# Row maxima of an attention kernel: a double-buffered tile, a later transposition, and a copy and a split on two other engines

## What is computed

```python
h = _layernorm(x, axis=-1) * (1 + ca) + sa
Q = _lora_linear(h, Wq, bq, Aq, Bq).reshape(N, S, HEADS, HEAD_DIM)      # K, V alike
energy = jnp.einsum('nqhd,nkhd->nhqk', Q, K) / jnp.sqrt(jnp.float32(HEAD_DIM))
attn = jax.nn.softmax(energy, axis=-1)
out = jnp.einsum('nhqk,nkhd->nqhd', attn, V).reshape(N, S, EMBED)
...
```

## Time and profile before

| | us |
|---|---|
| median of 3 runs (lowest, highest) | 1998.48 (1993.88, 2003.48) |
| the profiled execution: its own time | 2001.02 |
| the profiled execution: span of its instructions | 1999.3 |
| mean granted TensorE clock | 0.978 of full speed |
| busy PE, DVE, ACT, POOL | 94%, 79%, 59%, 16% |

### The profile page before, as it was taken

How to read it: one execution, slowest core, us unless ns; L and a number is a source line. 1 busy time by engine, 2 the same in 40 slices (tenths; PEclk the granted TensorE clock), 3 DMA queues, 4 the chain that set the end, 5 groups by cost and what they waited for, 6 DMA issues and landing times.

```text
span 1999.3 us, 33500 instructions
## 1 busy us (share of the span) xinstructions
PE 1883.2 (94%) x12334; PEld 705.1 (35%) x12335; DVE 1576.3 (79%) x2802; ACT 1179.2 (59%) x1354; POOL 322.2 (16%) x361
## 2 busy tenths in 40 slices
PE   7688999999999999999999999999975799999997
PEld 5332222222222222222222222222224555666664
DVE  4377999999999999999999999999816632254443
ACT  4534777777777777777777777777761221111111
POOL 5535000000000000000000000000016532323332
PEclk9898999999999999999999999999997799999999
DMA  4541111211111111111111111111056433222221
GB/s 152 169 148 37 41 41 50 64 44 41 41 60 57 39 41 55 58 46 38 42 60 56 42 38 53 56 43 38 11 171 214 139 106 116 95 78 71 68 66 47
DMA packets 89734, 141.48 MB, mean 71 GB/s; under 512 B 13104, under 2 KB 60208, under 8 KB 89472
## 3 DMA queue, kind: packets, MB, share of 16 engines
q1 hardware_dynamic: 74336, 102.01, 16.2%
q0 software_dynamic: 10240, 32.40, 4.9%
q10 hardware_dynamic: 5024, 5.24, 0.8%
HBM read 90.84 MB, written 48.51 MB: 70 GB/s over the span
## 4 chain that ended last, share of the span: by engine, by line
PE 83%; DVE 4%; issue 4%; POOL 3%; DMA 3%; ACT 1%; SPq 1%; POOLq 0%; DVEq 0%; ACTq 0%
PE ps L853 25%; PE ps L842 21%; PE ps L808 16%; PE ps L1514 7%; PE ps L1065 5%; PE ps L1532 3%; PE ps L1398 3%; DVE mx L909 2%; DMA l_in<-inverse_sums 2%; POOL parts L693 1%; ACT prob L947 1%; POOL rest L689 1%; PE ps L1523 1%; DMA qk_parts<-parts 1%; POOL k_low L681 1%
## 5 line engine op out<-in xcount | busy, mean ns | idle before, releaser
L909 DVE TENSOR_REDUCE mx<-ps 128x1 f32<-128x512 f32 x2048 | 1276.8, 682 | 47.4 <-PE ps L808 42.9
L947 ACT ACTIVATE prob<-ps 128x1024 f32<-128x1024 f32 x1024 | 992.3, 1021 | 294.6 <-PE ps L842 292.3
L853 PE MATMUL ps<-prob,vs 128*32 128x512 f32 x4096 | 546.4, 605 | 0.7 <-ACT prob L947 0.7
L808 PE MATMUL ps<-k_high,q_high 64*128 64x512 bf16 x2048 | 411.9, 388 | 32.4 <-DMA k_low<-qk_parts 17.5
L842 PE MATMUL ps<-q_high,k_high 64*128 64x512 bf16 x2048 | 389.6, 377 | 3.4 <-ACT prob L947 2.5
L842 PE MATMUL ps<-q_low,k_low 34*128 34x512 bf16 x2048 | 389.8, 377 | 0.0
L808 PEld LDWEIGHTS ps<-k_high,q_high 64*128 64x128 bf16 x2048 | 100.9, 92 | 670.6 <-DVE mx L909 603.7
L975 POOL COPY vs<-v_all 128x256 f32 (+1 forms) x32 | 12.7, 400 | 1138.3 <-PE ps L853 1138.2
L842 PEld LDWEIGHTS ps<-q_low,k_low 34*128 34x128 bf16 x2048 | 100.0, 94 | 117.5 <-issue 0.3
L1563 ACT ACTIVATE esig<-ps 128x512 f32<-128x512 f32 x39 | 23.3, 597 | 195.9 <-PE ps L1514 195.9
L842 PEld LDWEIGHTS ps<-q_high,k_high 64*128 64x128 bf16 x2048 | 101.4, 96 | 86.9 <-ACT prob L947 27.9
(11 more groups left out here) (145 smaller groups left out, 1312.4 us busy)
## 6 DMA issues: line engine op xcount, KB each, us to landing
k_high<-qk_parts SPq DMA_DIRECT2D x128, 128.0 KB
qk_parts<-parts SPq DMA_DIRECT2D x32, 384.0 KB, 3.6
q_high<-qk_parts SPq DMA_DIRECT2D x128, 64.0 KB
k_low<-qk_parts SPq DMA_DIRECT2D x128, 64.0 KB
head_out<-head_out_sb SPq DMA_DIRECT2D x32, 256.0 KB, 10.8
sorted_in<-zero_row POOLq DMA_DIRECT2D x13, 390.0 KB, 7.0
xs<-sorted_in SPq DMA_DIRECT2D x39, 130.0 KB
q_low<-qk_parts SPq DMA_DIRECT2D x128, 32.0 KB
```

The costliest lines, as they stand in the source:

```text
L808: pe.matmul(ps[:, ring_bank(2 * m + u), :], q_high[p][mine, t * P:(t + 1) * P], k_high[p][mine, c * CH:(c + 1) * CH], start=True, stop=Tru ...
L853: mm = pe.matmul(ps[32 * j:32 * j + 32, 7, :], vs[buf(h)][:, kt, :], prob[:, kt % 2, j * CH:(j + 1) * CH], start=(kt == 0), stop=(kt == KT ...
L909: dve.tensor_reduce(mx[:, at, c:c + 1], ps[:, ring_bank(k), :], AX.X, ALU.max).then_inc(s_ring, 1)
L947: act.activation(prob[:, kt % 2, :].rearrange("p (u c n) -> p u c n", u=2, c=2)[:, :, half, :], ps[:, 2 * half:2 * half + 2, :], ACT.Exp). ...
```

## The change

- `mx` becomes two tiles, used by heads in turn. DVE reduces unit 0 and unit 1 of the next head first and makes `mneg` of the finished head after them; it doesn't wait there for a write of its own.
- The transposition of the maxima moves from between units 0 and 1 of the next head to behind its third pair (`TURN_AT` = 2). Its place in the ring moves with it: after units 4 and 5.
- ACT copies the turned maxima out of PSUM into a new tile `turned_sb` (`take_turned`), behind the exponentials of step 12, and counts `s_turned`, which frees the place in the ring. GpSimd makes both rows of `mb` from that tile (`split_maxima`) and counts `s_mb`, for which SP waits.
- `LEAD` is 12. Two more pairs of head 1 stand beside the matmuls ahead of the first head, and pairs 0 and 1 of a head stand in step 11 instead of 12. The turn stays in step 12.
- The waits of the ring come from a table, the class `Ring`. `max_pair` calls `ring_place` once for each of its two units, and each call writes a wait of its own.
- The gates on GpSimd are written in parts, with the split of head 1 between them; the staging of the values, the weight loads and the zero fills are written out by head, each set ahead of a split.

```diff
-LEAD = 10
+LEAD = 12
...
 RING = 3
+TURN_AT = 2
...
+class Ring:
+
+
+    def __init__(self):
+        self.place, self.released = {}, []
+        count = {"dve": 0, "act": 0}
+        for n in range(NH + 1):
+            for m in range(PAIRS if n < NH else 0):
+                for u in range(2):
+                    self.add((n, m, u), "dve", count)
+                if n and m == TURN_AT:
+                    self.add((n - 1, "turned"), "act", count)
+        self.add((NH - 1, "turned"), "act", count)
+        self.total = count
+
+    def add(self, what, engine, count):
+        self.place[what] = len(self.released)
+        count[engine] += 1
+        self.released.append((engine, count[engine]))
+
+    def bank(self, what):
+        return 4 + self.place[what] % RING
+
+    def made(self, what):
+        return self.place[what] + 1
+
+    def taken(self, what):
+        return self.released[self.place[what]][1]
...
-        mx = r("mx", [P, KT, CPB])
+        mx = buffers("mx", [P, KT, CPB], F32, r)
...
                 p = buf(h)
-                sp.wait_ge(s_ring, MAXIMA * (num(h) + 1) + (1 if last else 2))
+                sp.wait_ge(s_mb, num(h) + 1)
...
+        ring = Ring()
+
+        def ring_place(pe, what):
+
+            at = ring.place[what]
+            if at >= RING:
+                engine, n = ring.released[at - RING]
+                pe.wait_ge(s_ring if engine == "dve" else s_turned, n)
+            return ps[:, ring.bank(what), :]
 
         def max_pair(pe, h, m):
 
-            p, t, c = buf(h), m // CPB, m % CPB
-
-            def unit(u):
+            p, n, t, c = buf(h), num(h), m // CPB, m % CPB
+            if m == 0:
+                pe.wait_ge(s_stack[p], STACK * (nth(h) + 1))
+            banks = [ring_place(pe, (n, m, u)) for u in range(2)]
+            for u in range(2):
                 mine = slice(u * HROWS, (u + 1) * HROWS)
-                pe.matmul(ps[:, ring_bank(2 * m + u), :], q_high[p][mine, t * P:(t + 1) * P],
+                pe.matmul(banks[u], q_high[p][mine, t * P:(t + 1) * P],
                           k_high[p][mine, c * CH:(c + 1) * CH], start=True, stop=True).then_inc(s_max, 1)
 
-            if m:
-                pe.wait_ge(s_ring, MAXIMA * num(h) + item(2 * m + 1) - RING + 1)
-                unit(0)
-                unit(1)
-                return
-            pe.wait_ge(s_stack[p], STACK * (nth(h) + 1))
-            if not first_head(h):
-                pe.wait_ge(s_ring, MAXIMA * num(h) - 1)
-            unit(0)
-            if not first_head(h):
-                turn_maxima(pe, plus(h, -1))
-            unit(1)
-
         def turn_maxima(pe, h):
+            bank = ring_place(pe, (num(h), "turned"))
             pe.wait_ge(s_neg, num(h) + 1)
-            pe.transpose(ps[0:KT, TURNED_BANK, 0:P], mneg[:, :], ident[:]).then_inc(s_max, 1)
+            pe.transpose(bank[0:KT, 0:P], mneg[:, :], ident[:]).then_inc(s_max, 1)
...
                     scores(*this, 1)
                     if beside:
                         max_pair(pe, who, first)
-                    elif first == 0 and after == 1:
-                        turn_maxima(pe, plus(h, 1))
+                    if first == TURN_AT and num(who) <= NH:
+                        turn_maxima(pe, plus(who, -1))
                     weigh(h, kt - 1)
                     if beside:
                         max_pair(pe, who, first + 1)
...
                 for m in range(n * LEAD // 4, (n + 1) * LEAD // 4):
                     if m:
                         max_pair(pe, (0, 1), m)
+                    if m == TURN_AT:
+                        turn_maxima(pe, (0, 0))
...
-        def reduce_pair(dve, step, h, m):
-
-            t, c = m // CPB, m % CPB
+        def reduce_pair(dve, h, m):
+
+            n, t, c = num(h), m // CPB, m % CPB
             for u in range(2):
-                k = 2 * m + u
-                if k == 1 and not first_head(h):
-                    turned_maxima(dve, step, plus(h, -1))
-                dve.wait_ge(s_max, 2 if first_head(h) and k == 0 else MAXIMA * num(h) + item(k) + 1)
+                what = (n, m, u)
                 at = u * HT + t
-                dve.tensor_reduce(mx[:, at, c:c + 1], ps[:, ring_bank(k), :], AX.X, ALU.max).then_inc(s_ring, 1)
-
-        def turned_maxima(dve, step, h, last=False):
-            dve.wait_ge(s_max, MAXIMA * (num(h) + 1) + (1 if last else 2))
-            dve.wait_ge(s_mrows[buf(h)], 64 * (nth(h) + 1))
-            turned = ps[0:KT, TURNED_BANK, 0:P]
-            step(dve.tensor_copy(mb[buf(h)][:, 0, :], turned))
-            dve.tensor_tensor(mb[buf(h)][:, 1, :], turned, mb[buf(h)][:, 0, :],
-                              ALU.subtract).then_inc(s_ring, 1)
+                dve.wait_ge(s_max, ring.made(what))
+                dve.tensor_reduce(mx[n % 2][:, at, c:c + 1], ps[:, ring.bank(what), :], AX.X,
+                                  ALU.max).then_inc(s_ring, 1)
 
         def attend_vector(dve, step):
-            def head(h, pairs=range(1, PAIRS), last=False):
-
-                for m in pairs:
-                    reduce_pair(dve, step, h, m)
-                dve.wait_ge(s_ring, MAXIMA * (num(h) + 1))
-                dve.tensor_reduce(mneg[:], mx[:], AX.X, ALU.max, negate=True).then_inc(s_neg, 1)
-                if last:
-                    turned_maxima(dve, step, h, last)
-                else:
-                    dve.wait_ge(s_neg, num(h) + 1)
-                    reduce_pair(dve, step, plus(h, 1), 0)
-
-            for p in range(NB):
-                dve.sem_inc(s_mrows[p], 64)
-            head((0, 0), pairs=())
+            def negate(n):
+
+                dve.wait_ge(s_ring, ring.taken((n, PAIRS - 1, 1)))
+                dve.tensor_reduce(mneg[:], mx[n % 2][:], AX.X, ALU.max, negate=True).then_inc(s_neg, 1)
+
             for n in range(1, NH):
-                head((0, n), last=n == NH - 1)
+                for m in range(PAIRS):
+                    reduce_pair(dve, (0, n), m)
+                    if m == 0:
+                        negate(n - 1)
+            negate(NH - 1)
             invert(dve, 0)
...
+            def take_turned(n):
+
+                what = (n, "turned")
+                act.wait_ge(s_max, ring.made(what))
+                wait(act, s_mb, n)
+                act.copy(turned_sb[:], ps[0:KT, ring.bank(what), 0:P]).then_inc(s_turned, 1)
...
+                if c * LEAD // 4 <= TURN_AT < (c + 1) * LEAD // 4:
+                    take_turned(0)
...
                     exps(n, kt)
                     if n and kt == 0:
                         head_copy(n - 1)
+                    if n + 1 < NH and LEAD + 2 * (kt - 1) == PAIRS + TURN_AT:
+                        take_turned(n + 1)
...
+            def split_maxima(n):
+
+                p = n % NB
+                pool.wait_ge(s_turned, n + 1)
+                pool.wait_ge(s_mrows[p], 64 * (n // NB + 1))
+                step(pool.tensor_copy(mb[p][:, 0, :], turned_sb[:]))
+                pool.tensor_tensor(mb[p][:, 1, :], turned_sb[:], mb[p][:, 0, :], ALU.subtract).then_inc(s_mb, 1)
+
+            def following(n):
+
+                pool.wait_ge(s_prob_free, AHEAD + KT * (n - 1))
+                stage((0, n + 1))
+                i, u = divmod(n + 1 - NB, NB)
+                if i < E and u < 2:
+                    dst, name = ((rgT, "rgT"), (ruT, "ruT"))[u]
+                    pool.dma_start(dst[:, bass.ds(i, 1)], io[name][:, bass.ds(i, 1)]).then_inc(s_expert, 16)
+                elif i < E:
+                    zero(i)
+                else:
+                    zero(n + 1 - NB * (E + 1) + E)
+
+            for p in range(NB):
+                pool.sem_inc(s_mrows[p], 64)
+            stage((0, 0))
+            split_maxima(0)
+            for n in range(1, NB):
                 stage((0, n))
             for o in range(UQ):
...
+            scale_modulation(pool, step)
+            gate(pool, step, 0)
+            split_maxima(1)
+            gate(pool, step, 3)
+            gate_bias(pool)
+            for n in range(2, NH):
+                if n + 1 < NH:
+                    following(n)
+                split_maxima(n)
```

More of the change, by code:

```diff
@@ L67 @@
 XW = D + TAGS
-MAXIMA = UNITS + 1
 RING = 3
+TURN_AT = 2
 NSC = 4
@@ L655, in beside @@
                         for _ in range(share[s]):
-                            reduce_pair(dve, step, (0, 0), next(units))
+                            reduce_pair(dve, (0, 0), next(units))
                 if more2:
@@ L778, in turn @@
                 if last >= 1:
-                    maxima(plus(h, 1), last == 1)
+                    maxima(plus(h, 1))
                 if last == 1:
@@ L976, in stage @@
                                  v_all[:, bass.ds(n // H * KT, KT), bass.ds(n % H * DH, DH)]).then_inc(s_vs, 1)
-            for n in range(NB):
-                stage((0, n))
-            for o in range(UQ):
-                pool.wait_ge(s_parts[o], 16 * (NCH + 1))
-            gates(pool, step)
```

(28 more changed lines are left out.)

28 lines of the change are left out of this document (13 added, 15 removed).

## The result

| | before | after |
|---|---|---|
| median (lowest, highest), us | 1997.74 (1993.88, 2003.48) | 2030.88 (2026.95, 2031.37) |
| ratio to before, 95% interval | | 1.0159 (1.0131 to 1.0187) |
| profiled execution: own time, span | 2001.02, 1999.3 | 2026.95, 2024.5 |
| step with pairs; period of a head | 2.49; 40.89 | 2.58; 41.84 |

What follows compares the result with a forecast made beforehand. The round trip PE to DVE to PE was taken as the bound. Second wait +44.1, passages -11.1, start +1.9, other pairs +1.5 and end -0.8 give +35.6 us on 1998.48: 2034 us, range 2014 to 2048.

Steps and rivals of the forecast that it cites:

- The bound and the second wait: Round trip PE to DVE to PE bounds; pair A's second wait adds 0.09 us a step, 490 times, +44.1 us.
- The passage: Between one head and the next: costs 0.68 us instead of 1.05, 30 times, -11.1 us.
- 0.26 (620.94 to 621.20) till the next start: Walk through step 11 on DVE: `mneg` delays pair B's first unit, starting at 1.89 instead of 1.74.
- The engines that take the work over: ACT copy, GpSimd split and SP transfers of the maxima: hidden with 2.4 us to spare, nothing added.
- Start, end: Ahead of the first scores +1.9 us; other pairs where PE waits for DVE +1.5; end of the attention -0.8.
- The second wait costs nothing: Rival, at each pair's waits: no cost, passage 0.64, -11.2 us, 1987 us; chance 0.10.
- Pair B pays too: Rival, at the pair behind the weighing: every pair pays, 490 x 0.09 more, 2078 us; chance 0.06.
- The maxima land late: Rival, copy, split and transfers: 1 us beyond the margin in all 30 heads, +30, 2064 us; chance 0.04.

Runs made afterwards that it cites:

- before_two_waits: The kernel before, with a second wait added in front of each pair from the second on, for the earlier unit's place: 2039.62 us, ratio 1.0213.
- one_wait: The changed kernel with one wait for both units of a pair, at the later unit's value (pairs 0 and 4 keep two): 1986.24 us, ratio 0.9941.
- second_wait_pair_b: As one_wait, but pairs of odd m (pair B, issued behind the weighing) keep both waits in the changed kernel's order: 1989.13 us, ratio 0.9953.
- waits_swapped: The changed kernel with both waits of each pair in the other order, the later unit's written first: 1987.35 us, ratio 0.9939.

## Why the prediction was right

**The bound and the second wait** were right, with their size. Forecast 0.09 a step, 490 times; measured 2.583 - 2.490 = 0.093, or 45.6 us in place of 44.1. The step shows in before_two_waits by itself and goes with one_wait. The cause was told less sharply than it is: the text asked how many waits a pair has, and what counts is which of them holds and where it stands. The text's own reading of the earlier trace rows had this: L838 in the kernel before was an extra wait, long met, that cost nothing. The Trainium skill (Perfetto Trace Analysis, Identifying Dependency Chains) speaks of instructions that wait on multiple engines, which is narrower than "more than one wait" in the prediction. The trace shows a semaphore instruction for two waits on one and the same semaphore too: most of the 1023 are such.

**The passage** was the term that was mis-sized: 0.68 forecast, 0.51 measured. The step of the working that failed is "0.26 (620.94 to 621.20) till the next start". That row was of a unit that waited for `s_neg`; the diff takes this wait away, and the walk kept its price. Without it `mneg` (631.34, 1.62 behind pair A, as forecast) lets the next unit start at 1.75, which is where an undisturbed one would. So pair 2 comes at 2.58 and not 2.72, and pair 3 at 4.43 and not 4.58. What holds pair 3 was right: it starts at 634.15 for its place in the ring, with DVE idle for 0.56 behind it. PE is through with the weighing at 634.02, 4.30 behind pair A and not 4.51, which costs nothing either way. The passage is worth 30 x 0.17 = 5.1 us, more than the miss; putting the wait back, on one_wait, gives 0.11 of the 0.17, and the rest was not traced.

**The engines that take the work over** did so unseen. ACT's copy starts 4.07 behind pair A and is through at 4.31 (forecast 4.6), the split at 5.16, SyncE's issues at 8.46 (forecast 5.4 and 8.1: the four issues took 3.28 and not 2.71). No row of PE's waits in the changed kernel names these transfers.

**Start, end, and what is not explained.** The first exponential starts at 181.8 instead of 179.8, +2.0 where 1.9 and part of 1.5 were forecast. By the spread above, from 180.3 to 185.1 with twelve pairs ahead, this agreement may be luck. The attention grew by 27.3, and 45.6 - 30 x 0.54 - 0.8 = 28.6 by the corrected terms; the 1.3 between them were not traced. From the last exponential to the end of the execution the changed kernel takes 517 us and the kernel before 521 in the profiled executions, without a change there; the other three runs of the changed kernel are 4 us longer than the profiled one. So the profiled executions are 25.9 us apart and the medians 33.1, against +35.6 forecast. That scatter made up for part of the mis-sized passage: that the time came within 3 us is in part luck.

**The rivals.** "The second wait costs nothing" is refuted by the step of 2.583; its 1987 is what the kernel takes once the waits are swapped (1987.35). "Pair B pays too" is refuted by the step of 2.583, which has room for one lag, and by the step of 2.490 in second_wait_pair_b, but for the one pair B that waits. "The maxima land late" did not happen with 12 pairs ahead; with 10 it begins.

## What to carry to other kernels

Find the round trip between engines before counting busy time, and look at each wait on it: where an instruction has several, write the one that is met last so that the instruction itself carries it (here: first), and let the ones that are long met stand ahead. When a duration is read as the distance to the next start, ask first what the next instruction waited for, above all if the change removes that wait. A new helper that waits once for each buffer may undo a hand-written merged wait without one line of arithmetic having changed.

## What the runs showed of the hardware

- With the holding wait in a semaphore instruction ahead, PE starts 0.09 us later than with it in the matmul: step 2.583 against 2.490, with 1023 such instructions on the line in either case. Once in a step of 2.5 us that is 3.7%. The row of the instruction starts 0.04 behind the release and lasts 0.05, and the matmul starts 0.056 behind its end; with the wait in the matmul it starts 0.056 behind the release.
- A semaphore instruction of 51 ns whose wait is met takes no time that shows: 573 or 1023 of them leave the step at 2.490. The profile shows 51 ns for those held by one release too, so the row's duration doesn't tell them apart; its start 0.04 behind the release does. The exception is pair 0 in waits_swapped, where one instruction has two of the waits: 30 rows span the hold and last 702 to 706 ns.
- On DVE a 128x64 reduction shows 0.21 us, but the next reduction starts 0.13 us behind its start, and 0.25 if it waits for the first one's release.
